# One Perceiver-style block on one core: another order on every queue, norms in parts, split products that wait part by part

## What is computed

```python
# 1: x += xattn(layernorm(x), context)
z = self_attn(x)                      # one head, causal and length mask, softmax(QK/sqrt(32)) V
x = layer_norm(x + z, ln1_g, ln1_b)
z = cross_attn(x, context)            # 2048 keys, length mask from counts of nonzero energies
x = layer_norm(x + z, ln2_g, ln2_b)
x = layer_norm(x + relu(x @ fc1_w + fc1_b) @ fc2_w + fc2_b, ln3_g, ln3_b)
# 2: x += rwkv(layernorm(x)); the 2 batches are 2 steps in time, 128 rows are the batch
r, wlog, k, v, a, g = (x + (xprev - x) * mu_m) @ W_m ...   # six mixes, six products
S = S * w + S (-kk)(kk * a)^T + v k^T ;  y = S r           # two steps only
y = group_norm(y) * lnx_w + lnx_b + (r * k * r_k).sum * v
h = layer_norm(inp + (y * g) @ Wo) ; out = layer_norm(silu(h @ Wf + bf))
# 3: x += ffn(layernorm(x)): attention of 8 heads x 64; values and outputs from 5 experts,
#    top 2 per head chosen by x @ Ws and x @ Wd, attention over the 128 rows
```

## Time and profile before

| | us |
|---|---|
| three runs | 268.88, 270.63, 265.19 (median 268.88) |
| the profiled execution | 267.06 |
| its span, first to last instruction | 265.3 |
| TensorE busy | 236.2 |
| VectorE busy | 172.2 |
| GpSimd busy | 101.1 |
| ScalarE busy | 87.3 |

### The profile page before, as it was taken

The page is one execution under the profiler, slowest core; times in us unless marked ns, Lnnn a source line. Parts: engine busy times, 40 slices in busy tenths (PEclk is TensorE's granted clock), DMA queues, the critical chain, the costliest instruction groups (busy, mean ns, idle before and its releaser), DMA issues.

```text
span 265.3 us, 3047 instructions
## 1 busy us (share of the span) xinstructions
PE 236.2 (89%) x1153; PEld 164.2 (62%) x1153; DVE 172.2 (65%) x309; ACT 87.3 (33%) x144; POOL 101.1 (38%) x81
## 2 busy tenths in 40 slices
PE   6899949899999998999889999998468769999895
PEld 5869538789878766677364444443134238899761
DVE  2216971469559996540846476899964686979781
ACT  2105420166077568312014445432000311240210
POOL 6002630159119936530411007599613422442000
PEclk9999977999999999999999999999959958999999
DMA  7999994000699997009900599000000000000002
GB/s 263 383 421 458 403 421 188 1 0 2 207 427 431 416 419 315 4 10 385 395 0 2 144 401 426 20 0 0 0 0 2 0 0 0 2 0 1 2 0 79
DMA packets 6350, 43.98 MB, mean 166 GB/s; under 512 B 832, under 2 KB 832, under 8 KB 1472
## 3 DMA queue, kind: packets, MB, share of 16 engines
q1 hardware_dynamic: 6336, 43.80, 41.0%
HBM read 43.27 MB, written 0.52 MB: 165 GB/s over the span
## 4 chain that ended last, share of the span: by engine, by line
PE 71%; DVE 15%; ACT 6%; POOL 3%; issue 2%; DMA 1%; DVEq 0%; ACTq 0%; POOLq 0%
PE psum L381 66%; ACT slots L1349 5%; PE psum L385 4%; POOL small L1592 2%; DVE ring_r L820 2%; DVE small L796 1%; DMA slots<-xin 1%; DVE slots L814 1%; DVE small L913 1%; POOL small L1688 1%; ACT ring_r L1349 1%; DVE slots L1251 1%; DVE slots L1267 1%; ACT slots_r L1349 1%; DVE slots L881 1%
## 5 line engine op out<-in xcount | busy, mean ns | idle before, releaser
L381 PE MATMUL psum<-ring,slots 128*128 128x512 f32 (+3 forms) x228 | 94.6, 567 | 4.9 <-ACT slots L1349 4.8
L381 PEld LDWEIGHTS psum<-ring,slots 128*128 128x128 f32 (+1 forms) x228 | 41.4, 199 | 49.4 <-issue 41.2
L1349 ACT ACTIVATE slots<-psum 128x512 f32<-128x512 f32 (+3 forms) x51 | 27.6, 551 | 115.4 <-PE psum L381 68.9
L1597 POOL TENSOR_TENSOR ring_r<-ring,ring_r 128x640 fp32r<-128x640 f32 x16 | 41.7, 2617 | 43.5 <-ACT ring_r L1349 43.4
L381 PE MATMUL psum<-slots,ring 128*128 128x128 f32 x448 | 54.8, 283 | 2.5 <-ACT slots L1349 2.1
L381 PEld LDWEIGHTS psum<-slots,ring 128*128 128x128 f32 x448 | 53.5, 199 | 4.8 <-ACT slots L1349 2.9
L381 PE MATMUL psum<-ring_r,slots_r 128*128 128x512 f32 x192 | 46.5, 397 | 1.1 <-ACT slots_r L1349 0.7
L381 PEld LDWEIGHTS psum<-ring_r,slots_r 128*128 128x128 f32 x192 | 35.4, 188 | 10.1 <-issue 2.2
L1592 POOL TENSOR_TENSOR small<-small,mhalf 128x1 f32<-128x1 f32 x16 | 14.9, 932 | 62.2 <-DVE small L800 62.2
L1349 ACT ACTIVATE ring_r<-ring 128x2048 fp32r<-128x2048 f32 (+1 forms) x17 | 31.7, 1865 | 14.3 <-PE psum L381 12.8
L820 DVE TENSOR_TENSOR ring_r<-ring,ring_r 128x1408 fp32r<-128x1408 f32 x16 | 29.9, 1872 | 5.0 <-ACT ring_r L1349 5.0
(11 more groups left out here) (156 smaller groups left out, 211.2 us busy)
## 6 DMA issues: line engine op xcount, KB each, us to landing
ring<-blocks SPq DMA_DIRECT2D x36, 1024.0 KB, 10.9
bc<-vecs SPq DMA_DIRECT2D x1, 3072.0 KB, 28.5
bc<-vecs SPq DMA_DIRECT2D x1, 1280.0 KB, 6.6
slots<-xin SPq DMA_DIRECT2D x2, 256.0 KB, 4.0
bc<-vecs SPq DMA_DIRECT2D x1, 512.0 KB, 10.2
y<-slots SPq DMA_DIRECT2D x2, 256.0 KB, 2.0
colv<-cols SPq DMA_DIRECT2D x1, 14.0 KB, 9.1
```

The costliest lines, as they stand in the source:

```text
L381: return t.matmul(o_, l, r, start=first, stop=last)
L1349: return a.activation(o, x, func, **kw)
L1597: g.tensor_tensor(ring_r[:, p, CUT:], ring[:, p, CUT:], ring_r[:, high(name), CUT:], ALU.subtract).then_inc(*split_lowg.inc(name))
```

## The change

No matmul, vector operation or transfer is added or removed, and no size changes. Three things change.

1. The order of the calls on all five queues, the fetches included.
2. `three` waits for the high part of the block first, for the low part of the activations before the second group of four, and for the block's low parts before the third. Before, it waited for all before its first matmul.
3. The helpers that held a whole norm (`add2`, `add3`, `out_o`, `out_s`) are cut into parts (`add2`, `norm2`, `done2` and so on), and `guard` is called apart from `penalty`, so that other work can stand between the parts. Some waits are written out that the old order implied.

```diff
-            def three(o_, xs, name, first, last):
+            def three(o_, xs, name, first, last, x_low):
 
                 s.wait_ge(*split_high.at(name))
-                s.wait_ge(*split_low.at(name))
-                s.wait_ge(*split_lowg.at(name))
                 ws = [ring_r[:, p, :].rearrange("p (c n) -> p c n", c=4) for p in (high(name), PLACE[name])]
                 pairs = [(xs[0], ws[0]), (xs[1], ws[0]), (xs[0], ws[1])]
                 for n, (x, w) in enumerate(pairs):
+                    if n == 1:
+                        s.wait_ge(*x_low)
+                    if n == 2:
+                        s.wait_ge(*split_low.at(name))
+                        s.wait_ge(*split_lowg.at(name))
...
                 s.wait_ge(*y_in[b].at("2"))
                 variance(b, "x2", Y[b], 1e-5)
+
+            def norm2(b):
                 s.wait_ge(s_bc1, 16)
                 centre(b, "x2", TMP[b], Y[b], "ln2_g")
+
+            def done2(b):
                 s.wait_ge(*turn[b].at("x1"))
                 affine(b, "x2", Z[b], TMP[b], "ln2_b")
...
             low("c12")
-            weigh2(1)
-            low("c13")
+            low("c11")
+            add2(0)
             p_split(1, 2)
             p_split(1, 3)
-            add2(0)
+            weigh2(1)
+            norm2(0)
+            done2(0)
+            low("c13")
             add2(1)
...
             out_o(1)
+            norm_h(1)
             silu(0)
+            affine(1, "h", hn[1], TMP[1], "norm_b")
             out_s(0)
...
             g.memset(mhalf[:, :], -0.5).then_inc(*const.inc("mhalf"))
+            g.memset(pick, 0.0).then_inc(*own_g.inc())
             g.memset(ident[:, :], 0.0).then_inc(*own_g.inc())
+            g.memset(causal[:, :], 0.0).then_inc(*own_g.inc())
...
+            g.memset(ones[:, :], 1.0).then_inc(*const.inc("ones"))
             deviation(0, "x")
...
             fetch("k1")
+            fetch("ct00")
             fetch("v1")
+            fetch("ct01")
```

More of the change, by code:

```diff
@@ L226, in build @@
         normed = flags("normed", LNS)
-        split_low = Flag(sem("split_low_dve"), SPLITS)
-        energy_in = flags("energy_read", ["n1", "len1", "nb1", "max1", "pT"])
+        split_low = Flag(sem("split_low_dve"), ["ct00", "ct01", "ct02", "ct03", "ct11", "ct10", "ct12", "ct13",
+                         "c00", "c01", "c02", "c03", "c10", "c12", "c11", "c13"])
+        energy_in = flags("energy_read", ["n1", "len1", "nb1", "pT", "lo", "max1"])
         k1_in = flags("k1_in", ["k1"])
@@ L249, in build @@
                       ["q1", "v1", "q2", "k2", "pc", "relu", "k", "th", "w", "r", "v", "g"])
[L250 to L253, removed]
+        exped = flags("exped", ["e1", "1", "0"], ["e1", "0", "1"])
+        split_high = Flag(sem("split_high"), ["ct00", "ct01", "ct02", "ct03", "ct10", "ct11", "ct12", "ct13", "c00",
+                          "c01", "c02", "c03", "c10", "c12", "c11", "c13"])
+        p_high = flags("p_high", ["0", "1", "3", "2"])
+        mixed = flags("mixed", ["k", "a", "v", "r", "g"], ["w", "g"])
         sq_a = flags("squared", ["vc"], ["kx", "a", "wexp", "vc"])
         silu_a = flags("silu", ["tanh"])
-        gates_a = flags("gates_act", ["xv", "w", "q", "k"])
+        gates_a = flags("gates_act", ["xv", "w", "k", "q"])
         exp_f = flags("exp_f", ["0", "1"])
@@ L610, in av @@
                 s.wait_ge(*val_v[b].at("vv"))
+                s.wait_ge(*exp_g[b].at("ones"))
                 if b:
@@ L1620, in _ @@
                             pattern=[[-1, 4], [0, 128]], channel_multiplier=1).then_inc(*const.inc("pick"))
[L1621 removed]
+            g.memset(ones[:, :], 1.0).then_inc(*const.inc("ones"))
             deviation(0, "x")
[L1623 to L1627 removed]
             deviation(1, "x")
             low("ct00")
+            deviation(0, "x1")
+            g.memset(tie[:, :, :], -TINY).then_inc(*own_g.inc())
+            g.memset(wbias[:, :], WC).then_inc(*const.inc("wbias"))
             low("ct01")
             low("ct02")
[L1632 removed]
             deviation(1, "x1")
[L1634 to L1640 removed]
+            low("ct03")
+            low("ct12")
+            low("ct10")
+            low("ct11")
+            low("ct13")
+            low("c00")
+            low("c01")
+            low("c02")
+            low("c03")
+            low("c10")
+            low("c11")
+            low("c12")
+            low("c13")
+            deviation(0, "x2")
+            s.wait_ge(*normed[0].at("x2"))
+            s.wait_ge(s_bc1, 16)
+            mul(x2b[0], Z[0], vec("fc2_b"), x2b_g[0], "x2b", ALU.add)
+            deviation(1, "x2")
+            s.wait_ge(*normed[1].at("x2"))
+            s.wait_ge(s_bc1, 16)
+            mul(x2b[1], Z[1], vec("fc2_b"), x2b_g[1], "x2b", ALU.add)
             deviation(0, "x3")
```

602 lines of the change are left out of this document (329 added, 273 removed), and 3 rows, old and new, of the table prod.

## The result

Four executions of the changed kernel have a median of 259.97 us (256.62 to 260.21), beside 267.79 us for the kernel before: ratio 0.970, 95% interval 0.964 to 0.976. Six more in a later run (f1_after_again) gave 256.66 us, ratio 0.960 (0.957 to 0.963). Executions of one kernel differ by several us with the clock that TensorE is granted, so times are read beside their mean granted clock (as a share of 2.4 GHz, after "at a clock of"), and stages from one profiled execution each.

The account below looks back on a forecast made before the run. TensorE, busy 89% of the span, was taken as the bound, with idle and half-clock time to recover. Terms +1.7 - 6.7 + 2.0 - 2.4 - 0.2 - 1.5 = -7.1 give span 258.2, time 260.0 us; range 256 to 267.

Parts of the forecast that it names:

- the head: Before q1: the memset of `ones` comes later, so the warm-up matmuls start at about 3.9 instead of 1.78; +1.7 us.
- the MLP: From f1(0) to step a(0): two bias matmuls move behind and relu(1) is covered, less new waits; -2.4 us.
- g(1) behind GpSimd's queue: Mixing step g(1) waits for mixg behind pv(1) and sc(0): idle 3.5 us, g(1) takes 5.1, ends 3.8 later.
- the wait for h(1): Before the transposes of h(1), after ro(1): affine(1, h) stands behind silu(0) on VectorE; idle 2.1 us.
- the steps up to ro(1): Step a(0) to the end of ro(1): steps, biases, g and yg together; -0.2 us.
- Self-attention: Through the first four scores: short waits, the 2.8 us idle before x1(0)'s transposes and its half clock go; -6.7 us.
- the scores and gathers: After the fourth score to f1(0): new waits for low parts outweigh 2.0 us saved; +2.0 us, bounds +0.5 to +4.
- GpSimd's 2.9 us per subtraction: In scores and gathers: a GpSimd subtraction beside VectorE's takes 2.9 us instead of 1.54 alone.
- the stall of VectorE for the deviation of x2(0): Last gather: done2(0) waits on VectorE for GpSimd's deviation, so the last group comes about 1.9 us late.
- The tail: Behind the last product: new places of fo and swapped output transfers leave its 7.7 us as it is; 0 to -1.
- a second behind h(1): Rival: the clock falls once more at h(1)'s transposes, fg(0) or rf(1) costs 2.3 us more: 262.3 us; chance 0.17.
- the experts: Last norms and experts, after ro(1): fg(0) at full clock and gate products starting earlier, less later turned h(1); -1.5 us.

Follow-up runs that it names:

- e1: Changed kernel with the memset of `ones` back right behind the select of `ident`, ahead of causal, kidx and pick: 258.88 us, ratio 0.964.
- e2: Changed kernel with ScalarE's mix for g ahead of evicting v(1), and GpSimd's mixg behind c1: 257.48, 262.16, 263.02 and 263.04 us.
- e3: Changed kernel with affine(1, h) ahead of silu(0) on VectorE and silu(1)'s tanh ahead of the copy of n5(0) on ScalarE: 264.82 us, ratio 0.989.
- e4: Changed kernel with the old wait, each split product waiting for all parts before its first matmul: 261.60, 264.19, 267.08 and 271.06 us.
- e6: Changed kernel with fo(0,2), its eviction, last addition and output transfer of batch 0 ahead of those of batch 1: 256.40 us, ratio 0.958.
- e9: Changed kernel with both the early memset of `ones` and fo(0,2) with output 0 ahead of batch 1's: 255.78 us, ratio 0.954.
- e7: Changed kernel with 1024 instead of 640 of each subtraction's 2048 columns on GpSimd, 1024 instead of 1408 on VectorE: 266.31 us, ratio 0.995.
- f3: Changed kernel with all low parts awaited before the second product group, the first group free of that wait: 265.08 us, ratio 0.986.
- f2: Changed kernel with `ones` early and the sums, fo and outputs at the end in the earlier kernel's order: 258.94 us, ratio 0.964.

## Why the prediction was right, and where it was not

- **Right, with its working:** the head (+1.8 for +1.7), the MLP (-2.3 for -2.4), g(1) behind GpSimd's queue (idle 2.9 and 5.16 us, for 3.5 and 5.1), the wait for h(1) (2.08 for 2.1), the steps up to ro(1) (-0.2). e1, e2 and e3 show the three waits to be what they were named. The 5.16 holds for this execution: in e1, e4, e6 and e9 g(1) took 3.70 behind the same idle.
- **Self-attention, -6.0 for -6.7.** The idle of 2.8 and the half clock near 36 went; .86 of a wait for the norm stayed, which the forecast had at nothing. No run takes this part of the order back, so its cause rests on the two timelines alone, as does the end of the 5.2 us wait of the earlier trace rows.
- **The term that was mis-sized: the scores and gathers, +2.0 forecast, -3.4 measured.** Two steps failed. The first: "Splitting the wait in `three` ... saves at the first score only the k2 split"; for the later scores and the gathers the sum gives the split wait nothing. With the old wait the new order costs 2.1 us in this stage (e4), close to my +2.0, though by chance, since the prices under the second step are not in it (e4's subtractions take 2.0 us each, and its VectorE does not stall); the split wait hides the late parts under groups of 1 us and turns the stage into -3.4. I had priced the lateness of the low parts in full, not less the cover of the groups that no longer wait. The second: GpSimd's 2.9 us per subtraction, and the stall of VectorE for the deviation of x2(0), 1.9; neither came. After, the timelines of POOL and DVE have:

```profile
99.50 6.05 POOL L1657 TENSOR_TENSOR ring_r<-ring,ring_r 128x640 fp32r<-128x640 f32 x3 [8.93 <-ACT ring_r L1407]
105.51 0.55 POOL L1652 TENSOR_TENSOR small<-small,mhalf 128x1 f32<-128x1 f32 x1
```

```profile
99.46 1.63 DVE L832 TENSOR_TENSOR ring_r<-ring,ring_r 128x1408 fp32r<-128x1408 f32 x1 [0.67 <-ACT ring_r L1407]
...
106.69 0.75 DVE L826 SCALAR_TENSOR_TENSOR slots<-slots,small,bc 128x512 f32<-128x512 f32 x1
```

Three subtractions take 6.05, which is one of 3.0 beside VectorE's and two of 1.5 free of it; the deviation is done at 106.06, and VectorE goes on with the norm's last operation at 106.69 without a stall. In all 16 subtractions take 2.0 us each (before 2.6).
- **The tail, +1.1 for 0 to -1.** Measured from the last gate product it grew: the gates end 6.8 us after the start of the last gather instead of 7.3, and behind that start TensorE, full from 239 to the end, has 15.6 us of work instead of 15.0 (52 matmuls instead of 44). Where the next engine has a backlog, the time behind a product's end is no term of its own: in both kernels TensorE's queue sets the end, not VectorE's last gate product.
- **The clock.** The forecast counted one fall for g(1) and had a second behind h(1) as a rival, at +2.3. It came: rf(1) takes 5.40 instead of 3.70, fg(0) keeps its 2.95. But it cost the path .6, not 1.7 or 2.3, because TensorE would have waited for n5(0) next. e7, where rf(1) kept 3.70, shows that: the transposes of n5(0) wait .89, and fg(0) starts 17.8 us after ro(1) instead of 18.4. The forecast had that wait at 1.1 in its own working and did not set it against the price of its rival. So the experts' -1.4 for -1.5 holds a fall that the sum left out, and most of it was covered. The slow start of q1(0), which the forecast named and left out of its sum, came in e4 and f3, at 1.8 and 2.0 us.

That the first median, 259.97, stands on the forecast, 260.0, is luck. The middle came 5.4 better, self-attention .7 and the tail 1.1 worse, which makes 256.6, the time of the executions at a clock of .986 (and the median of f1). Those at .971, three of the first four, are 3.4 longer. None of them was profiled; e1's profile at .971 would fit, with g(1) at full clock (-1.46) and 21.5 instead of 16.6 us from the sums before the last gather to the end, the first 10 of them at half clock. Why the clock falls in the experts in some executions and not in others was not settled.

## What to carry to other kernels

A wait in front of a group of matmuls is worth splitting where parts of its operands come later than others, and a new order should be judged with the waits it will have: here order and split wait are worth -3.4 us together in the stage of scores and gathers, +2.1 and -0.9 alone. Taking a wait of 2 to 3 us away by moving work forward in a queue moved it to the next product (e2, e3): ask what is ready next before ending a wait. And place what the first instruction waits for first: 1.4 us in the head stayed as far as the last gather (f2). Last, a forecast can meet the median and miss one of its terms by 5 us; only the checkpoints showed it.

## What the runs showed of the hardware

- A GpSimd subtraction that starts together with VectorE's (.05 us behind it) takes 2.98 us, one alone 1.54, while VectorE's then keeps its 1.63. Where VectorE's starts while GpSimd's runs, it is the one that grows, to 1.83 to 2.13 us (2.09 at 64.11). Rows of DVE and POOL of the kernel before:

```profile
98.41 1.63 DVE L820 TENSOR_TENSOR ring_r<-ring,ring_r 128x1408 fp32r<-128x1408 f32 x1 [0.27 <-ACT ring_r L1349]
98.46 2.98 POOL L1597 TENSOR_TENSOR ring_r<-ring,ring_r 128x640 fp32r<-128x640 f32 x1 [2.51 <-ACT ring_r L1349]
```

1.54 + 1.63 - .05 is 3.12, near 2.98: as if GpSimd started when VectorE is done. The Trainium skill (SBUF — State Buffer, "Who interferes with whom") says just that of two inputs read from SBUF; by that rule the price belongs to subtractions that overlap, not to all of them, and the trace agrees: 2.98 in this pair, 1.53 to 1.6 where the queues were apart.
- q1(0) is slower in some executions than in others whose instructions up to there are the same: 64 matmuls in 7.41 (the change), 9.25 (e4) and 9.40 us (f3), with the warm-up at 3.90 in all three. The clock of the profile does not show it. From 9.2 to 11.0 us TensorE gets through 15 matmuls in the change and 8 in e4, and the row gives the granted clock as 1.00 in both (windows of the change, then of e4):

```profile
9.20:11.00 1.80, 1.77 (x15) 1.77 (x16) 0.04 (x1) 0.00 (x0) 0.00 (x0) 1.00 1.02 432
9.20:11.00 1.80, 1.77 (x8) 1.78 (x9) 0.00 (x0) 0.00 (x0) 0.00 (x0) 1.00 1.02 432
```

That is noise of 2 us in any comparison of single executions.
- The granted clock fell behind waits of 2.1 (h(1)), 2.6, 2.8 and 2.9 us (to a mean of .70 from 176.5 to 181.6 and .75 from 198.3 to 205.0 in the change), in e3 and e7 also behind one of 1.6 us, but not always: in e1, e4, e6 and e9 g(1) took 3.70 us behind the same 2.9 us of idle that cost the change 1.46 (in e9 at a clock of 1.00).
